# Two decoder-style layers on one core: the last tile's end on the VectorE, an expert merge by its transpose, and unread filler matmuls

## The chip, the cores and the metric

One core of a Trainium2 chip runs the whole program. The metric is the device time of one execution in microseconds (us), the median over runs. TensorE (PE) multiplies and transposes, VectorE (DVE) and GpSimd (POOL) do elementwise work, ScalarE (ACT) activations and copies, SyncE (SP) issues the stores. Each engine runs its instructions in the order in which the program lists them, and waits on semaphores where it must. GpSimd doesn't touch PSUM in this kernel.

## The reference

The input x has 4 batches of 512 tokens with 128 features; the context has 77 keys a batch.

```python
x = x + xattn0(layernorm(x), ctx, ctx, mask)      # 16 heads of 8, softmax over 77 keys, projection, biases
x = x + ffn0(layernorm(x))                        # 4-head attention over the batch axis, LN, 8-expert top-1 MoE with capacity, LN
x = x + xattn1(layernorm(x), ctx, ctx)            # 16 heads, only the 32 largest scores of 77 enter the softmax, values = ctx
x = x + ffn1(layernorm(x))                        # out = sigmoid(xr @ Wr.T) * (relu(xk @ Wk.T)**2 @ Wv.T), xr and xk mix a token with the one before
```

In the MoE an expert is two linear maps with no nonlinearity between them: `h = disp @ w1 + b1`, `y = h @ w2 + b2`. So an expert is one 128x128 matrix w1 @ w2 and one bias b1 @ w2 + b2. In xattn1 the cutoff is the 32nd largest score of a row, and `scores >= cutoff` stay.

## The kernel before

The 2048 tokens are 16 tiles of 128 (t = 4 * batch + j). The first half of the program works on the four tiles of one j at a time: `attend` (the first cross attention), `among` (attention over the batch axis, LN, the gate's logits) and `gates` (the place of a token in its expert, which needs the counts of the tiles before; for j = 3 those of all). The second half works by single tiles: `experts` (nine products with the merged experts, scaled on ScalarE and summed on TensorE), `query` and `kept` (LN, the queries, the scores in psS, their copy to SBUF), `topk`, `weigh`, `value` and `mix`.

Each engine's program is a set of small steps such as `max01@5`. The list `ORDER` names all steps of all engines in one row; `run` goes through it and emits, on each engine, the steps that this engine has. So the list alone decides what is queued behind what. Semaphores carry the data dependences, and `begun` counts in the list how many steps have used a PSUM bank before a given one.

`topk` of a tile is four rounds on the DVE: max (L897, 16 MAX8, one a head, the eight largest of 77) and, between them, mark (L905, MATCH_REPLACE8, which takes them out). `free` (L912) copies the largest of round 1 to mxc, `ends` (L916) the 32nd value. Then `weigh`: `dif` (L394, POOL) takes the maximum off the scores, `exp` (L582, ACT), `cut` (L400, POOL) takes the cutoff off, `sign` (L586, L588, ACT: sign, then relu) makes 0 or 1 of it, `product` (L407, POOL) multiplies both. `dif` waits for mx_copied, which `ends` sets, though it reads only what `free` wrote. `turn0` to `turn2` (L1184) transpose the 1232 weights of a token in ten chunks, `copy0` to `copy2` bring them to SBUF, `value` (L1198) multiplies with the context, `norm` (L925, L928, DVE) divides by the sum, `add3` (L417, POOL) adds x2. `mix`: `sum4`, `square4`, `scale4`, `norm4` are the LN on ACT and POOL with zf as result; `fturn` (L1211), `shift`, `up` (L1216 to L1219, four products), `acts`, `down` (L1223), `fvalue` (L627, ACT, a copy out of PSUM), `half` and `end` (L428, L431, POOL). SP stores fin.

The merge of the experts stands in j = 0: `wa0` to `wa7` (L1045) multiply w1 and w2 of an expert in four pieces of K = 128, `w12c` copies four results, and `bb0` to `bb7` (L1056) make b1 @ w2 of all experts with a weight matrix b1z that has one column set for each, 32 matmuls; `b12c` (L742) adds b2.

The product with the mask row (L978) has bf16 operands `mones` (ones) and `mrow` (the fill values, zero where the key is allowed).

## Time and profile before

| | us |
|---|---|
| median of three runs | 627.32 |
| the runs | 620.28, 627.32, 627.65 |
| the profiled execution | 621.48 |
| its span, first to last instruction | 619.7 |
| busy: PE, DVE, ACT, POOL | 424.8, 498.3, 284.2, 264.3 |

The profile is of one execution. Times in it count from the start of its span. "Busy" is the time in which an engine works; an instruction's idle time is the gap ahead of it, with what ended it. PEclk is the granted TensorE clock as a share of 2.4 GHz. An fp32 matmul stands as two records.

### The profile page before, as it was taken

How to read it: one execution, taken by the hardware profiler on the slowest of the kernel's cores; microseconds unless marked ns; L12 is line 12 of the kernel's file. 1: busy time of each engine (PE TensorE's matmuls, PEld its weight loads, DVE VectorE, ACT ScalarE, POOL GpSimd, SP SyncE). 2: the span in 40 equal slices, each digit the busy share in tenths (PEclk: the TensorE clock that was granted, in tenths of full speed). 3: DMA queues.
4: the chain of work that ended last, by engine and by line, in shares of the span. 5: the costliest groups of instructions: out<-in, count | busy, mean ns of one | idle time of the engine just before them, and what ended most of it. 6: DMA issues, size and time to landing. Idle time of an engine off the chain costs nothing.

```text
span 619.7 us, 10123 instructions
## 1 busy us (share of the span) xinstructions
PE 424.8 (69%) x2376; PEld 320.2 (52%) x2376; DVE 498.3 (80%) x3052; ACT 284.2 (46%) x786; POOL 264.3 (43%) x396
## 2 busy tenths in 40 slices
PE   4589987787777748236775876866797687455634
PEld 3359756674666435125654545655565465344523
DVE  5844669949587898989759999999989999989900
ACT  2214122324333224313675677666847766642342
POOL 4400300410240073523574476656747755663361
PEclk9669996969699577655878579877956886655555
DMA  8500000000000000000000000000000000000000
GB/s 285 223 1 1 1 2 1 1 0 2 2 1 1 2 1 1 0 2 1 1 5 5 2 6 5 2 5 6 5 2 5 6 2 5 5 6 5 5 2 8
DMA packets 6075, 9.56 MB, mean 15 GB/s; under 512 B 888, under 2 KB 5120, under 8 KB 5760
## 3 DMA queue, kind: packets, MB, share of 16 engines
q1 hardware_dynamic: 5728, 8.35, 3.8%
q10 hardware_dynamic: 288, 0.56, 0.3%
q8 instruction: 20, 0.33, 0.2%
q14 instruction: 39, 0.32, 0.2%
HBM read 7.86 MB, written 1.05 MB: 14 GB/s over the span
## 4 chain that ended last, share of the span: by engine, by line
PE 38%; DVE 18%; POOL 14%; ACT 14%; issue 14%; DMA 1%; SPq 0%; POOLq 0%; ACTq 0%; DVEq 0%
PE psM L1007 5%; PE psM L1150 4%; POOL dif L394 3%; PE psM L1198 3%; ACT area_b L586 3%; PE psM L1142 3%; POOL area_b L400 3%; PE psT L1184 3%; DVE area_b L905 2%; POOL p L407 2%; ACT mparts L545 2%; DVE d L673 2%; PE psM L1078 2%; DVE top L897 2%; PE psS L975 2%
## 5 line engine op out<-in xcount | busy, mean ns | idle before, releaser
L897 DVE MAX8 top<-area_b 128x8 f32<-128x77 f32 x768 | 112.3, 223 | 0.0
L905 DVE MATCH_REPLACE8 area_b<-top,area_b 128x77 f32<-128x77 f32 x512 | 106.8, 223 | 0.0
L307 POOL TENSOR_TENSOR rstd_m<-veps_m,expo 128x4 f32<-128x4 f32 x8 | 8.2, 1019 | 114.5 <-DVE veps_m L641 114.5
L1184 PE MATMUL psT<-consts,p 128*128 128x128 f32 (+1 forms) x160 | 37.7, 369 | 24.5 <-POOL p L407 18.8
L1007 PE MATMUL psM<-vblk,pT 128*128 128x81 f32 (+1 forms) x320 | 46.5, 309 | 10.4 <-DVE x L694 5.8
L905 DVE MATCH_REPLACE8 area_b<-top,area_a 128x77 f32<-128x77 f32 x256 | 53.5, 223 | 0.0
L407 POOL TENSOR_TENSOR p<-area_b 128x1232 f32<-128x1232 f32 x16 | 45.6, 2851 | 17.7 <-issue 13.2
L1198 PE MATMUL psM<-vblk,pT 128*128 128x81 f32 (+1 forms) x320 | 49.3, 321 | 4.6 <-ACT pT L600 4.2
L1198 PEld LDWEIGHTS psM<-vblk,pT 128*128 128x128 f32 (+1 forms) x320 | 48.0, 237 | 8.5 <-issue 7.1
L1007 PEld LDWEIGHTS psM<-vblk,pT 128*128 128x128 f32 (+1 forms) x320 | 45.4, 227 | 12.9 <-issue 12.5
L394 POOL TENSOR_TENSOR dif<-area_a,mxc 128x1232 f32<-128x1232 f32 x16 | 36.0, 2247 | 37.5 <-DVE mxc L916 37.5
L897 DVE MAX8 top<-area_a 128x8 f32<-128x77 f32 x256 | 37.5, 224 | 11.8 <-ACT area_a L574 11.4
L1142 PE MATMUL psM<-w,y1T 128*128 128x512 f32 (+1 forms) x64 | 32.7, 601 | 19.6 <-ACT mparts L545 19.4
L1184 PEld LDWEIGHTS psT<-consts,p 128*128 128x128 f32 (+1 forms) x160 | 24.9, 185 | 40.1 <-POOL p L407 23.6
L545 ACT ACTIVATE mparts<-psM,cur 128x128 f32<-128x128 f32 x128 | 38.0, 367 | 13.9 <-PE psM L1142 13.7
L1150 PE MATMUL psM<-mparts,consts 128*128 128x128 f32 x288 | 41.4, 307 | 0.0
L905 DVE MATCH_VALUE_LOAD area_b<-top,area_b 128x8 f32 x512 | 40.8, 80 | 0.0
L1150 PEld LDWEIGHTS psM<-mparts,consts 128*128 128x128 f32 x288 | 40.5, 226 | 0.0
L470 ACT ACTIVATE pT<-psT 128x512 f32<-128x512 f32 x16 | 9.6, 597 | 58.4 <-PE psM L1007 31.6
L400 POOL TENSOR_TENSOR area_b<-area_a,mxc 128x1232 f32<-128x1232 f32 x16 | 36.0, 2247 | 0.6
L582 ACT ACTIVATE area_b<-dif 128x1232 f32<-128x1232 f32 x16 | 19.7, 1230 | 33.6 <-POOL dif L394 33.5
L668 DVE TENSOR_REDUCE mx<-psS 128x16 f32<-128x1232 f32 x16 | 23.0, 1436 | 12.3 <-PE psS L978 12.3
(210 smaller groups left out, 1058.3 us busy)
## 6 DMA issues: line engine op xcount, KB each, us to landing
area_a<-in_w1T SPq DMA_DIRECT2D x1, 2048.0 KB, 10.7
area_b<-in_w SPq DMA_DIRECT2D x1, 2048.0 KB, 14.4
x<-in_x SPq DMA_DIRECT2D x4, 256.0 KB, 6.9
out<-fin SPq DMA_DIRECT2D x16, 64.0 KB, 1.5
rows<-in_rows SPq DMA_DIRECT2D x1, 576.0 KB, 7.5
vblk<-in_vblk SPq DMA_DIRECT2D x1, 540.0 KB, 15.2
weights<-in_weights SPq DMA_DIRECT2D x1, 516.0 KB, 6.6
consts<-in_consts ACTq DMA_DIRECT2D x1, 392.5 KB, 4.0
```

The source lines that it names most:

```text
L394: e.tensor_tensor(dif[:], scores_sb[t % RING][:], mxc[:, t % RING, 0, :, None].broadcast_to([P, H, KEYS]), ALU.subtract)\
L400: e.tensor_tensor(cut, scores_sb[t % RING][:], mxc[:, t % RING, 1, :, None].broadcast_to([P, H, KEYS]), ALU.subtract)\
L407: e.tensor_tensor(p1.rearrange("p (h k) -> p h k", k=KEYS), ex1, cut, ALU.mult).then_inc(s["p_set"], 1)
L545: ins = e.activation(mparts[:, x_], psM0[:, at + (x_ - lo) * D:at + (x_ - lo + 1) * D], ACT.Copy, scale=cur[:, D + x_:D + x_ + 1])
L668: e.tensor_reduce(mx0.rearrange("p (g i) -> p g i", g=G), scores_ps, AX, ALU.max).then_inc(s["s_max"], 1)
L897: ins = e.max(top[:, r, h], (left if r else scores_sb[t % RING])[:, h])
L905: ins = e.match_replace(left[:, h], top[:, r, h], (left if r else scores_sb[t % RING])[:, h], GONE)
L1007: ins = mm(pvs0[:, :, FIRST[c] * VE:FIRST[c] * VE + VB], pT[0:w, c], vblk0[0:w, b, c, None, :].broadcast_to([w, COPIES, VB]), start=(c == ...
L1142: mm(psM0[:, 0:(hi - lo) * D], y1T[:], w12[:, lo:hi].rearrange("p e n -> p (e n)"), start=True, stop=True)\
L1150: ins = mm(psM0[:, 0:D], ident, mparts[:, x_], start=False, stop=(x_ == E))
L1184: ins = tr(psT[0:w, 0, (c % 4) * P:(c % 4 + 1) * P], p1[:, c * P:c * P + w], ident)
L1198: ins = mm(pvs1[:, :, FIRST[c] * VE:FIRST[c] * VE + VB], pT1[0:w, c], vblk1[0:w, t // NJ, c, None, :].broadcast_to([w, COPIES, VB]), start ...
```

## The change

- **The last tile's end.** For t = 15 (`LASTT`) the steps `ends`, `cut`, `sign` and `product` are gone. Instead the DVE has `part0` to `part3`, four SCALAR_TENSOR_TENSOR each, `p = (score >= cutoff) * exp`, which read the cutoff straight from the fourth round of max. add3 and the LN of this tile go to the DVE (`close`: add, bn_stats, bn_aggr, add of epsilon; `closen`), with the power on POOL (`root`), and `end` reads the product from PSUM on the DVE, so that `fvalue` is gone for it.
- **dif.** It waits for S_read, set by `free`, and stands right behind `free` in the list; `cut` waits for mx_copied.
- **The merge by its transpose.** `wa` makes (w1 @ w2) transposed with b1 @ w2 as a 129th column, in three groups that ACT copies (`wt0` to `wt2`); `wu0`, `wu1` transpose four experts each back, `bu` the eight bias columns. b1z, b1T, its DMA and `bb` are gone. w1T carries b1 as a further row, made ahead on the host with the layout of the arrays.
- **Fillers.** `fill@0` to `fill@166` and `stoke@167` to `stoke@206` are each two matmuls with the operands of the mask row, whose result nothing reads. `fill` writes psT's second bank, and waits for the copies of what was there; `stoke` writes psS's last bank, once all scores are kept.
- **The list.** ORDER is written anew for all steps, before as much as after the places where the steps above stand.

The diff, with the parts cut that only delete declarations; of the list a line of either stands.

```diff
...
+LASTT = NT - 1
...
+FILLS = 167
+STOKES = 40
...
                 def a():
-                    hold(e, s["mx_copied"], t + 1)
+                    hold(e, s["S_read"], t + 1)
                     hold(e, s["exp_set"], t)
...
                     hold(e, s["p_set"], t)
+                    hold(e, s["mx_copied"], t + 1)
                     e.tensor_tensor(cut, scores_sb[t % RING][:], mxc[:, t % RING, 1, :, None].broadcast_to([P, H, KEYS]), ALU.subtract)\
...
 
-                return dict(dif=a, cut=b, product=c)
+                return dict(dif=a, cut=b, product=c) if t < LASTT else dict(dif=a)
 
...
                     e.tensor_tensor(x3[:, t % 2], x2[:, t % 8], att1[:], ALU.add).then_inc(s["x3_set"], 1)
-                return dict(add3=d)
+
+                def root():
+                    hold(e, s["z_step"], 3)
+                    e.tensor_tensor(rstd["m"][:, 0:1], veps["m"][:, 0:1], expo[:, 0:1], ALU.pow).then_inc(s["z_root"], 1)
+                return dict(add3=d) if t < LASTT else dict(root=root)
 
...
                     e.tensor_tensor(fin[:], x3[:, t % 2], vv, ALU.add).then_inc(s["f_fin"], 1)
-                return dict(scale4=ln_scalars(2, t, s["n4_sq"], s["n4_step"], s["n4_nm"]), half=one, end=end)
+                return dict(scale4=ln_scalars(2, t, s["n4_sq"], s["n4_step"], s["n4_nm"]), half=one, end=end) if t < LASTT else dict(half=one)
             run(e, attend=attend, among=among, experts=experts, query=query, weigh=weigh, value=value, mix=mix)
...
                 if j == 0:
+                    for n in range(3):
+                        def aside(n=n):
+                            lo, hi = 3 * n, min(3 * n + 3, E)
+                            e.wait_ge(s["w12_made"], n + 1)
+                            e.activation(w12t[:, lo:hi].rearrange("p e n -> p (e n)"), psM1[:, 0:(hi - lo) * (D + 1)], ACT.Copy)\
+                                .then_inc(s["w12t_copied"], 1)
+                        steps[f"wt{n}"] = aside
                     for n in range(2):
                         def keep(n=n):
-                            e.wait_ge(s["w12_made"], n + 1)
+                            e.wait_ge(s["w12_turned"], n + 1)
                             e.activation(w12[:, 4 * n:4 * n + 4].rearrange("p e n -> p (e n)"), psM1, ACT.Copy).then_inc(s["w12_stored"], 1)
...
                     return f
-                return dict(exp=a, sign=b, copy0=c(0), copy1=c(1), copy2=c(2))
+                steps = dict(exp=a, copy0=c(0), copy1=c(1), copy2=c(2))
+                if t < LASTT:
+                    steps.update(sign=b)
+                return steps
 
...
                     e.activation(vv, psT[:, 1, 3 * P:4 * P], ACT.Copy).then_inc(s["f_vv"], 1)
-                return dict(sum4=a1, square4=a2, norm4=a3, shift=shift, acts=acts, fvalue=value)
+                steps = dict(shift=shift, acts=acts)
+                if t < LASTT:
+                    steps.update(sum4=a1, square4=a2, norm4=a3, fvalue=value)
+                return steps
             run(e, attend=attend, among=among, experts=experts, query=query, kept=kept, weigh=weigh, mix=mix)
...
                 steps.update({f"mark{r}{g}": mark(r, g) for r in range(rounds - 1) for g in range(G)})
-                steps.update(free=free, ends=ends)
+                steps.update(free=free)
+                if t < LASTT:
+                    steps.update(ends=ends)
+                    return steps
+
+                def part(g):
+                    def f():
+                        hold(e, s["exp_set"], t + 1)
+                        hold(e, s["p_turned"], 3 * t)
+                        hold(e, s["topk_step"], last(2 * rounds - 2) + 1 + g)
+                        for h in range(g * HG, g * HG + HG):
+                            ins = e.scalar_tensor_tensor(p1[:, h * KEYS:(h + 1) * KEYS], scores_sb[t % RING][:, h], top[:, rounds - 1, h, 7:8],
+                                                         ex1[:, h], ALU.is_ge, ALU.mult)
+                        ins.then_inc(s["p_part"], 1)
+                    return f
+                steps.update({f"part{g}": part(g) for g in range(G)})
                 return steps
...
                                     rden1[:, :, None].broadcast_to([P, H, HD]), ALU.mult).then_inc(s["a_norm"], 1)
-                return dict(norm=a)
-            run(e, attend=attend, among=among, gates=gates, topk=topk, value=value)
+
+                def close():
+                    hold(e, s["f_fin"], t - 1)
+                    hold(e, s["n4_out"], t)
+                    hold(e, s["a_norm"], t + 1)
+                    e.tensor_tensor(x3[:, t % 2], x2[:, t % 8], att1[:], ALU.add).then_inc(s["x3_set"], 1)
+                    hold(e, s["x3_set"], t + 1)
+                    e.bn_stats(stats["m"][:, 0], x3[:, t % 2]).then_inc(s["z_step"], 1)
+                    hold(e, s["z_step"], 1)
+                    e.bn_aggr(mv["m"][:, 0], stats["m"][:, 0]).then_inc(s["z_step"], 1)
+                    hold(e, s["z_step"], 2)
+                    e.tensor_scalar(veps["m"][:, 0:1], mv["m"][:, 0, 1:2], EPS, None, ALU.add).then_inc(s["z_step"], 1)
+
+                def norm():
+                    hold(e, s["z_root"], 1)
+                    hold(e, s["f_turned"], t)
+                    e.tensor_scalar(zf, x3[:, t % 2], mv["m"][:, 0, 0:1], rstd["m"][:, 0:1], ALU.subtract, ALU.mult).then_inc(s["n4_out"], 1)
+                return dict(norm=a) if t < LASTT else dict(norm=a, close=close, closen=norm)
+
+            def mix(t):
+                def end():
+                    hold(e, s["f_one"], t + 1)
+                    hold(e, s["f_v"], t + 1)
+                    hold(e, s["f_fin"], t)
+                    e.tensor_tensor(vv, psT[:, 1, 3 * P:4 * P], er, ALU.mult).then_inc(s["f_mul"], 1)
+                    hold(e, s["f_mul"], t + 1)
+                    hold(e, s["stored"], 16 * t)
+                    e.tensor_tensor(fin[:], x3[:, t % 2], vv, ALU.add).then_inc(s["f_fin"], 1)
+                return dict(end=end) if t == LASTT else {}
+            run(e, attend=attend, among=among, gates=gates, topk=topk, value=value, mix=mix)
 
...
                                 e.wait_ge(s["v_masked"], 2 * B)
-                            if x_ == 4:
-                                e.wait_ge(s["w12_stored"], 1)
+                            if x_ % 3 == 0:
+                                hold(e, s["w12t_copied"], x_ // 3)
                             for c in range(FC):
-                                ins = mm(psM1[:, (x_ % 4) * D:(x_ % 4 + 1) * D], w1T[:, c, x_], w2[:, c, x_], start=(c == 0), stop=(c == FC - 1))
-                            if x_ % 4 == 3:
+                                ins = mm(psM1[:, x_ % 3 * (D + 1):(x_ % 3 + 1) * (D + 1)], w2[:, c, x_], w1T[:, c, x_],
+                                         start=(c == 0), stop=(c == FC - 1))
+                            if x_ in (2, 5, 7):
                                 ins.then_inc(s["w12_made"], 1)
...
 
-                    def bias(x_):
+                    def upright(n):
                         def f():
-                            if x_ == 0:
-                                e.wait_ge(s["w12_stored"], 2)
-                                e.wait_ge(s["b1_spread"], 1)
-                            for c in range(FC):
-                                ins = mm(psM1[0:E, 0:D], b1z[:, c, x_ * E:(x_ + 1) * E], w2[:, c, x_],
-                                         start=(x_ == 0 and c == 0), stop=(x_ == E - 1 and c == FC - 1))
-                            if x_ == E - 1:
-                                ins.then_inc(s["b12_made"], 1)
-                                e.wait_ge(s["weights_in"], 16)
+                            e.wait_ge(s["w12t_copied"], 3)
+                            hold(e, s["w12_stored"], n)
+                            for x_ in range(4):
+                                ins = tr(psM1[:, x_ * D:(x_ + 1) * D], w12t[:, 4 * n + x_, 0:D], ident)
+                            ins.then_inc(s["w12_turned"], 1)
                         return f
+
+                    def bias():
+                        e.wait_ge(s["w12_stored"], 2)
+                        tr(psM1[0:E, 0:D], w12t[:, :, D], ident).then_inc(s["b12_made"], 1)
+                        e.wait_ge(s["weights_in"], 16)
                     steps.update({f"vb{n}": spread(n) for n in range(2)}, **{f"wa{x_}": merged(x_) for x_ in range(E)},
-                                 **{f"bb{x_}": bias(x_) for x_ in range(E)})
+                                 **{f"wu{n}": upright(n) for n in range(2)}, bu=bias)
                 return steps
...
                     def f():
+                        if t == LASTT:
+                            hold(e, s["p_part"], min(2 * g + 2, G))
                         if g == 0:
-                            hold(e, s["p_set"], t + 1)
+                            hold(e, s["p_set"], min(t + 1, LASTT))
                             hold(e, s["t_copiedA"], 3 * begun(f"turn0@{t}", "ta0", "ta1", "ta2", "ta3"))
...
                     hold(e, s["t_copiedV"], begun(f"fturn@{t}", "tb0", "tb1", "tb2", "tb3"))
-                    hold(e, s["b1_spread"], 6)
+                    hold(e, s["mix_set"], 5)
                     tr(psT[:, 1, 0:P], zf, ident).then_inc(s["f_turned"], 1)
...
                 return dict(fturn=turn, up=up, down=down)
-            run(e, attend=attend, among=among, gates=gates, experts=experts, query=query, weigh=weigh, value=value, mix=mix)
+            def warm(k):
+                def stream(bank):
+                    for _ in range(2):
+                        mm(bank[:, 0:B * KEYS], mones[:], mrow.rearrange("p b k -> p (b k)"), start=True, stop=True)
+
+                def between():
+                    hold(e, s["v_masked"], 2 * B)
+                    hold(e, s["t_copiedV"], begun(f"fill@{k}", "tb0", "tb1", "tb2", "tb3"))
+                    hold(e, s["f_vv"], begun(f"fill@{k}", "fturn"))
+                    stream(psT[:, 1])
+
+                def after():
+                    hold(e, s["S_kept"], NT)
+                    stream(psS[:, G - 1])
+                return dict(fill=between) if k < FILLS else dict(stoke=after)
+            run(e, attend=attend, among=among, gates=gates, experts=experts, query=query, weigh=weigh, value=value, mix=mix, warm=warm)
 
...
 INDICES = dict(attend=range(NJ), among=range(NJ), gates=range(NJ), experts=range(NT), query=range(NT), kept=range(NT), topk=range(NT),
-               weigh=range(NT), value=range(NT), mix=range(NT))
-ORDER = """hstats@0 masks@0 hrstd@0 kblk1@0 hnorm@0 vb0@0 kblk@0 vb1@0 bias@0 vm0@0 hturn@0 hstats@1 keys@0 hT@0 vm1@0 hq@0 hrstd@1 wmix@0
-hqT@0 s0@0 hnorm@1 hstats@2 bias@1 hturn@1 hT@1 mx0@0 hq@1 hrstd@2 hnorm@2 sub0@0 bias@2 hstats@3 s1@0 exp0@0 hrstd@3 ta0@0 mx1@0
...
-keep@15 max00@14 dif@13 max01@14 sum4@12 max02@14 square4@12 max03@14 mark00@14 cut@13 exp@13 mark01@14 mark02@14 mark03@14
+mark13@15 exp@15 turn2@14 max20@15 copy2@14 max21@15 value@14 max22@15 max23@15 mark20@15 mark21@15 mark22@15 mark23@15 max30@15
...
         consts=consts, early=early, weights=weights, cols=cols, rows=rows, vblk1=laid.transpose(1, 2, 0, 3, 4).reshape(P, B, NCH, VB),
-        b1T=a["L0_ffn_b1"].reshape(E, FC, P).transpose(2, 1, 0),
         b2=a["L0_ffn_b2"],
-        w1T=a["L0_ffn_w1"].reshape(E, D, FC, P).transpose(3, 2, 0, 1),
+        w1T=np.concatenate([a["L0_ffn_w1"], a["L0_ffn_b1"][:, None, :]], axis=1).reshape(E, D + 1, FC, P).transpose(3, 2, 0, 1),
         w2=a["L0_ffn_w2"].reshape(E, FC, P, D).transpose(2, 1, 0, 3),
...
```

Three places of the list, as it comes out on an engine. First GpSimd (POOL) over one tile in the full stretch near the end; L400 (after: L401) is cut, L394 dif, L407 (L408) product, L417 (L418) add3, L359 to L363 scale4, L423 to L431 (L428 to L436) the end of the tile before. Before:

```order
L394 TENSOR_TENSOR dif<-area_a,mxc 128x1232
L417 TENSOR_TENSOR x<-x,att 128x128
L400 TENSOR_TENSOR area_b<-area_a,mxc 128x1232
L359 TENSOR_SCALAR lvar<-lsq 128x1
L361 TENSOR_TENSOR lrs<-lvar,expo 128x1
L363 TENSOR_TENSOR lnm<-lneg,lrs 128x1
L407 TENSOR_TENSOR p<-area_b 128x1232
L423 TENSOR_SCALAR er<-er 128x128
```

And now:

```order
L418 TENSOR_TENSOR x<-x,att 128x128
L401 TENSOR_TENSOR area_b<-area_a,mxc 128x1232
L359 TENSOR_SCALAR lvar<-lsq 128x1
L361 TENSOR_TENSOR lrs<-lvar,expo 128x1
L363 TENSOR_TENSOR lnm<-lneg,lrs 128x1
L408 TENSOR_TENSOR p<-area_b 128x1232
L428 TENSOR_SCALAR er<-er 128x128
L394 TENSOR_TENSOR dif<-area_a,mxc 128x1232
```

dif moved from ahead of the cut to behind the product; it is the next tile's dif there.

The DVE at the end of the program, before (L897 max, L905 mark, L925 and L928 norm, L916 ends):

```order
L905 MATCH_REPLACE area_b<-top,area_b 128x77 x16
L897 MAX top<-area_b 128x8 x16
L925 RECIPROCAL rden<-psM 128x16
L928 TENSOR_TENSOR att<-psM,rden 128x128
L916 COPY mxc<-top 128x16
L925 RECIPROCAL rden<-psM 128x16
L928 TENSOR_TENSOR att<-psM,rden 128x128
```

And now (L946 the parts, L966 to L977 close and closen, L985 and L988 end):

```order
L913 MAX top<-area_b 128x8 x8
L946 SCALAR_TENSOR_TENSOR p<-area_a,top,area_b 128x77 x4
L913 MAX top<-area_b 128x8 x8
L956 RECIPROCAL rden<-psM 128x16
L959 TENSOR_TENSOR att<-psM,rden 128x128
L946 SCALAR_TENSOR_TENSOR p<-area_a,top,area_b 128x77 x12
L956 RECIPROCAL rden<-psM 128x16
L959 TENSOR_TENSOR att<-psM,rden 128x128
L966 TENSOR_TENSOR x<-x,att 128x128
L968 BN_STATS stats_m<-x 128x6
```

The first part stands between two groups of max, the other three behind tile 14's norm.

TensorE around the routing of j = 3, before (L950 the turns, L1089 and L1100 products of `among`, L1118 and L1119 places, L1198 value of tile 0, L1127 and L1128 tile 3's turn):

```order
L950 MATMUL psM<-consts,oo 128x128 x4
L1089 MATMUL psM<-weights,mT 128x128 x4
L950 MATMUL psM<-consts,y1s 128x128 x4
L1100 MATMUL psM<-weights,mT 128x8 x4
L1118 MATMUL psM<-oh,consts 128x104
L1119 MATMUL psM<-seen_odd,ones 128x104
L1198 MATMUL psM<-vblk,pT 128x3x27 x10
L1127 MATMUL psM<-consts,cur 128x128
```

And now (L1291 the fillers):

```order
L1009 MATMUL psM<-consts,oo 128x128 x4
L1291 MATMUL psT<-mrow,mones 128x308 x6
L1150 MATMUL psM<-weights,mT 128x128 x4
L1291 MATMUL psT<-mrow,mones 128x308 x52
L1009 MATMUL psM<-consts,y1s 128x128 x4
L1291 MATMUL psT<-mrow,mones 128x308 x4
L1161 MATMUL psM<-weights,mT 128x8 x4
L1291 MATMUL psT<-mrow,mones 128x308 x28
L1179 MATMUL psM<-oh,consts 128x104
L1180 MATMUL psM<-seen_odd,ones 128x104
```

The same steps in the same order, with 45 pairs between them.

## Rows read from the trace of the kernel before

**Rows 1.** Windows of the whole span; columns as "us, PE PEld DVE ACT POOL busy (x), PEclk, DMA share, GB/s".

```profile
0.00:19.00 19.00, 9.12 (x50) 6.25 (x50) 11.20 (x41) 3.99 (x6) 9.30 (x23) 1.00 0.90 313
19.00:43.00 24.00, 16.30 (x69) 9.89 (x70) 16.59 (x40) 4.78 (x7) 5.76 (x11) 0.51 0.19 81
43.00:98.00 55.00, 48.66 (x389) 38.97 (x388) 33.73 (x64) 17.22 (x35) 5.64 (x10) 1.00 0.00 1
98.00:299.00 201.00, 137.81 (x726) 102.20 (x727) 165.93 (x718) 65.14 (x165) 59.55 (x75) 0.73 0.00 1
299.00:317.00 18.00, 12.27 (x80) 9.40 (x80) 7.74 (x63) 13.26 (x41) 11.17 (x17) 0.88 0.02 5
317.00:588.00 271.00, 187.99 (x1013) 143.59 (x1013) 261.94 (x2126) 169.05 (x506) 160.48 (x245) 0.73 0.02 4
588.00:619.70 31.70, 12.66 (x56) 9.85 (x55) 1.18 (x5) 10.73 (x29) 12.38 (x17) 0.55 0.02 5
```

**Rows 2.** Waits: engine, line, waited for; us in total, times, longest.

```profile
DVE rden L925 <- PE psM L1198: 25.6, 6, 18.5
...
DVE top L897 <- ACT area_a L574: 11.4, 2, 10.2
```

**Rows 3.** Timeline of the end: start us, us, engine, line, operation [idle before, releaser].

```profile
588.71 0.26 DVE L925 RECIPROCAL rden<-psM 128x16 f32<-128x16 f32 x1 [0.96 <-PE psM L1198]
...
589.46 2.25 POOL L394 TENSOR_TENSOR dif<-area_a,mxc 128x1232 f32<-128x1232 f32 x1 [7.15 <-DVE mxc L916]
...
597.38 0.47 PE L1211 MATMUL psT<-consts,zf 128*128 128x128 f32 x1 [8.70 <-ACT zf L526]
...
600.09 1.06 PE L1184 MATMUL psT<-consts,p 128*128 128x128 f32 x4
...
601.90 1.11 PE L1184 MATMUL psT<-consts,p 128*128 128x128 f32 x4
...
604.87 3.00 PE L1198 MATMUL psM<-vblk,pT 128*128 128x81 f32 x20 [0.73 <-ACT pT L600]
607.91 0.26 DVE L925 RECIPROCAL rden<-psM 128x16 f32<-128x16 f32 x1 [18.53 <-PE psM L1198]
...
611.84 0.48 PE L1211 MATMUL psT<-consts,zf 128*128 128x128 f32 x1 [3.97 <-ACT zf L526]
...
616.32 0.28 ACT L627 ACTIVATE vv<-psT 128x128 f32<-128x128 f32 x1 [0.89 <-PE psT L1223]
...
617.27 0.45 POOL L431 TENSOR_TENSOR fin<-x,vv 128x128 f32<-128x128 f32 x1
```

**Rows 4.** The page's groups (busy us, mean ns), and one round of max, tile 14's.

```profile
L905 DVE MATCH_REPLACE8 area_b<-top,area_b 128x77 f32<-128x77 f32 x512 | 106.8, 223 | 0.0
...
568.44 2.34 DVE L897 MAX8 top<-area_a 128x8 f32<-128x77 f32 x16
```

**Rows 5.** The group of the freeing copy, and the timeline around it, tiles 12 and 15.

```profile
L912 DVE COPY mxc<-top 128x16 f32<-128x16 f32 x16 | 8.6, 539 | 0.4
...
509.00 2.25 POOL L400 TENSOR_TENSOR area_b<-area_a,mxc 128x1232 f32<-128x1232 f32 x1
...
509.55 1.73 DVE L912 COPY mxc<-top 128x16 f32<-128x16 f32 x1
...
568.48 2.25 POOL L394 TENSOR_TENSOR dif<-area_a,mxc 128x1232 f32<-128x1232 f32 x1 [7.15 <-DVE mxc L916]
...
574.20 0.17 DVE L912 COPY mxc<-top 128x16 f32<-128x16 f32 x1
...
576.10 2.79 POOL L407 TENSOR_TENSOR p<-area_b 128x1232 f32<-128x1232 f32 x1 [1.57 <-issue]
```

**Rows 6.** Timeline of TensorE: the mask row's four matmuls at either clock.

```profile
40.21 1.21 PE L978 MATMUL psS<-mrow,mones 65*128 65x308 bf16 x4
...
50.65 0.70 PE L978 MATMUL psS<-mrow,mones 65*128 65x308 bf16 x4
```

**Rows 7.** The group of the bias products in the merge.

```profile
L1056 PE MATMUL psM<-area_b,b1z 128*8 128x128 f32 x64 | 7.5, 273 | 0.0
```

253 lines of the change are left out of this document (132 added, 121 removed).

## The prediction

> **What bounds the kernel now.** I read the table of windows first, then the list of waits, the timeline of the last 32 us, and then the rows of single instructions. In the windows the VectorE (DVE) is the engine to follow [rows 1]: it is busy for 498.3 of 619.7 us, and the 121.4 us in which it is not are 7.8 up to 19 us, 7.4 up to 43, 21.3 up to 98, 35.1 up to 299, 10.3 up to 317, only 9.1 in the 271 us of 317 to 588, and 30.5 at the end. So three things can shorten the program: a shorter end, fewer stalls ahead of 317 us, and fewer in the full stretch. TensorE is the reason for most stalls ahead of 299 us, and its granted clock says how it ran there: 0.51 in 19 to 43 and 0.73 in 98 to 299, where 0.5 is 1.2 GHz and 1.0 is 2.4 GHz.
>
> The waits name two places [rows 2]. The DVE waited 25.6 us for the product with the values (L1198), of which 18.5 is the last tile's and 7.1 are five waits of earlier tiles. It waited 10.2 us once for tile 3's scores: these need the routing of the last quarter, and only tile 2's top-k lies beside that chain.
>
> The end is a pure chain [rows 3]. The last MAX8 ends at 587.75 (the reciprocal at 588.71 less its 0.96 of idle); then come dif 589.46, first transposes 600.09, value 604.87, norm 607.91, turn of zf 611.84, copy of v 616.32, last add 617.27, end 619.7.
>
> **Part 1, the last tile's end.** Gone for tile 15: the copy of the cutoffs, the GpSimd's cut and product, ScalarE's sign and relu; dif and exp stand earlier, under the rounds of max. New: sixteen SCALAR_TENSOR_TENSOR on the DVE. The trace has none of 77 columns; below it stands MAX8, 2.34 us for 16 (0.146 each), above it MATCH_REPLACE8 with 106.8/512 = 0.209 [rows 4]. I take 0.16, the price nearest to a plain pass over 77 columns, with the ends 0.146 and 0.21 (2.3 to 3.4 us for all). Call M the end of the last MAX8. The first four now lie ahead of M (0.65 us later). Behind M: norm of tile 14 0.6, twelve parts 1.9. The first transposes need two parts: M+1.3, against M+12.3 before. The second group stood 1.8 behind the first [rows 3]: M+3.1 to M+4.2. Then tile 14's turn, the two last transposes (M+5.4) and, in front of value now, tile 14's four products (eight passes, 2 us at the 1.06 for four [rows 3]): value starts at M+7.5 instead of M+17.1. That is 9.6 less the 0.65, and I take off 0.9 because value may run at the low clock. The norm behind it goes by bn_stats, bn_aggr, an add, one GpSimd power and one DVE instruction, some 2.8 us instead of 611.84 - 607.91 = 3.9, and the last multiply reads PSUM on the DVE: 0.8 less. Sum: **-10**, bounds -7 to -12.
>
> **Part 2, dif ahead of the cutoff.** dif (2.25 us) waits for S_read instead of mx_copied, so behind the cutoffs only cut, sign, relu and product remain. The five waits of 7.1 us were at most 2.5 us long by the 25.6 less 18.5 [rows 2]; a chain 2.25 us shorter removes nearly all of them: **-5.5**, bounds 0 and -7.
>
> **Part 3, what it collides with.** The copy that frees the scores (L912) took 539 ns in the mean, 16 of them 8.6 us, though an undisturbed one takes 0.17: 5.9 us were lost. The rows of 509 us show how: GpSimd's cut runs from 509.00 to 511.25, the DVE's copy from 509.55 to 511.28 [rows 5]. The copy ends when the GpSimd instruction ends, and the DVE stands. In the last tiles of before the copy came at 574.20 and the product at 576.10, so they missed each other. With dif (started 568.48) gone from the front, the product starts some 2.3 us earlier, about 573.8, and runs for 2.8 us over the place of the copy: 2.0 to 2.4 us of stall in a tile. By the order of steps product@t-1 stands ahead of free@t for t = 5 and 9 to 15, eight tiles; for the others it stands behind. 8 x 1.6 = 13 less the 5.9 that are there: **+7**. Bounds: -6 (nothing collides) and +20 (thirteen tiles at 2.0, less 5.9). The Trainium skill says the same of the mechanism ("SBUF — State Buffer", Who interferes with whom): GpSimd and the DVE's second port pair are one lock, held for the whole instruction, and an fp32 copy may take it. It adds that who issues first wins. By that rule the product, issued first, blocks the copy, and the trace agrees with 1.73 against 0.17.
>
> **Part 4, fillers.** 167 pairs in psT's second bank, 40 in psS's last. The operands are those of the mask row, whose four matmuls took 1.21 us at the low and 0.70 at the high clock [rows 6]; so a pair costs about 0.6 or 0.35, and less where they follow each other. They cost nothing where TensorE would have waited, and cost their full time where the next instruction's operands are already there: TensorE goes in order. In 19 to 43 us TensorE was busy 16.3 of 24 us at 0.51 [rows 1]; at the high clock that is some 9.5, and the DVE's 7.4 of idle can fall by half: **-3.5** (0 to -6). In 98 to 299 the DVE idles 35.1 us at a mean clock of 0.73; a mean of 0.73 over two levels means 54% of the time at the low one, and that is where products take twice as long. I take **-8** (0 to -18). Tile 3's scores: products of some 13 us of TensorE at the low clock stand in that chain; half of that is 6, of which 5 shorten the 10.2: **-5** (0 to -10). Where a pair is in the way: TensorE's list has fillers at 38 places ahead of the last four tiles; if at twelve of them the operands come while a pair at the low clock is halfway, that is 12 x 0.3: **+4** (0 to +15). The last 34 pairs stand between value@11 and fturn@11; before, TensorE idled 8.7 us ahead of tile 14's turn of zf, the same place of a tile [rows 3]; they take 68 x 0.13 to 0.26 us. At the high price they'd delay tile 11's end by several us, but the top-k of tile 13 covers it: counted in the +4. None stands in the last three tiles, so the end isn't warmed by them.
>
> **Part 5, the merge.** 64 recorded passes of 7.5 us in one row go [rows 7], nine transposes and three ScalarE copies come, TensorE is left with some 5 us less in 43 to 98, where the DVE idles 21.3 us: **-3** (+1 to -5). One DMA less, one larger by 1/128, a memset and a small copy less: nothing, since the weights aren't waited for.
>
> **Sum.** -10 - 5.5 + 7 - 3.5 - 8 - 5 + 4 - 3 = -24, against the profiled execution's 621.5: 597.5. Its 621.5 stands 5.8 below the median of the three runs (627.3), which spread by 7.4. Moved by -24 the median would be 603.3. I forecast 600.
>
> **The rivals.**
> A. *The copies are blocked nearly everywhere and the clock gives little.* For: each steady tile has the same 6 us between the cutoffs and the next copy [rows 5]. Against: in tiles 6 to 8 the product stands behind. Part 3 at +16, part 4 at -8: about 614.
> B. *The clock gives what its stretches promise.* Part 4 at -28 and the chain of tile 3 gone, part 3 as forecast: 586. For: the two lowest clocks stand where the DVE idles. Against: shorter TensorE steps uncover ScalarE and GpSimd steps.
> C. *Only the end.* The order of steps brings ahead of 588 us as much as it takes (-10 alone): 611.5 by the profiled execution, 617 by the median, so about 2%.
> D. *Slower: pairs of fillers at the low clock in front of waiting steps.* If the clock doesn't follow, 167 pairs at 0.6 are 100 us of TensorE instead of 58, in order with the products that the DVE waits for. Part 4's gains (16.5) vanish and of the 100 us more than 40 would have to fall on the chain: 597.5 + 16.5 + 36 = 650. It decides from the point where the fillers delay the DVE by more than 20 us in all. Against: TensorE is idle for 63 of the 201 us of 98 to 299 [rows 1].
>
> **How the numbers follow.** Forecast 0.52, A 0.15, B 0.2, C 0.1, D 0.03. A measurement of this kernel can tell about 2% from no change, so faster means below 614.8. All of forecast and B, and half of A and C, lie below that: 0.85; within 2% 0.12; slower 0.03. The range takes in B and the nearer side of A: 585 to 616.
>
> **What would show it.** Right: the last MAX8 to the end 22 us instead of 32; copies of L928 (free) of 1.5 to 2.5 us in tiles 9 to 15 that end with GpSimd's product; no wait of norm over 0.5 us in the full stretch; granted clock over 0.9 in 215 to 317; the wait for tile 3's scores at 5 or less. Wrong: DVE idle ahead of 317 us above 80 (fillers in the way), or a steady tile that takes less than 20.7 us (no collision).

## The result, and the profile after

| | before | after |
|---|---|---|
| median, us | 626.1 (620.3, 627.3, 627.7, 624.9) | 639.18 (634.69, 642.47, 641.95, 636.42) |
| the profiled execution, its span | 621.48, 619.7 | 634.69, 632.8 |
| ratio | | 1.0268 [1.0213, 1.0322] |

The changed kernel is slower, by 2.7%; the forecast was 600, with 585 to 616 as its range. Medians here are over all runs of a kernel, ratios leave disturbed runs out, so the two need not agree to the last digit.

The same windows as [rows 1], with the borders moved to where the same work now stands:

```profile
0.00:19.00 19.00, 10.81 (x48) 7.23 (x49) 11.68 (x43) 3.99 (x6) 9.77 (x23) 0.86 0.91 320
19.00:43.00 24.00, 21.93 (x89) 11.86 (x87) 14.71 (x35) 4.09 (x7) 5.11 (x10) 0.50 0.18 75
43.00:98.00 55.00, 49.07 (x357) 41.33 (x358) 36.83 (x71) 19.56 (x40) 6.51 (x10) 0.90 0.00 1
98.00:299.00 201.00, 170.39 (x999) 124.11 (x999) 174.20 (x767) 68.39 (x175) 64.18 (x80) 0.82 0.00 1
299.00:335.00 36.00, 30.09 (x189) 20.64 (x189) 24.12 (x198) 24.55 (x82) 22.18 (x40) 0.95 0.02 5
335.00:600.00 265.00, 189.56 (x986) 142.92 (x984) 230.80 (x1854) 154.24 (x450) 146.98 (x217) 0.73 0.01 4
600.00:632.80 32.80, 18.21 (x74) 15.40 (x74) 16.23 (x110) 7.17 (x24) 4.63 (x11) 0.50 0.02 6
```

The sixth row tells the story. In 335 to 600 us the VectorE (DVE) is busy for 230.8 of 265 us, so it stands for 34.2; in the full stretch of before it stood for 9.1 of 271. The waits say for what, against 25.6, 6, 18.5 in [rows 2]:

```profile
DVE rden L956 <- PE psM L1261: 43.5, 8, 11.9
```

8.96 us of it is the last tile's; 34.5 is in other tiles, 2.1 at tile 1 and 32.4 behind ends@4. To date it, take the start of the copy of the cutoffs (`ends@t`), once a tile:

| `ends` of tile | 2 | 4 | 5 | 6 | 8 | 9 | 10 | 14 |
|---|---|---|---|---|---|---|---|---|
| before | 306.1 | 355.7 | 376.7 | 397.1 | 437.8 | 460.6 | 481.5 | 568.2 |
| after | 300.5 | 350.6 | 374.4 | 406.4 | 446.1 | 474.3 | 502.9 | 588.0 |

At tile 4 the changed kernel is 5.1 us ahead, at tile 14 it is 19.8 behind: 24.9 us are lost between them, all of it in the tiles that end at 374.4, 406.4, 474.3 and 502.9; the others take some 20 to 22 us as before. The end itself, timeline from the last MAX8 on (columns as in [rows 3]):

```profile
608.64 0.91 DVE L946 SCALAR_TENSOR_TENSOR p<-area_a,top,area_b 128x77 f32<-128x77 f32 x4
...
610.59 0.24 DVE L956 RECIPROCAL rden<-psM 128x16 f32<-128x16 f32 x1
...
611.07 2.79 DVE L946 SCALAR_TENSOR_TENSOR p<-area_a,top,area_b 128x77 f32<-128x77 f32 x12
...
612.25 1.12 PE L1247 MATMUL psT<-consts,p 128*128 128x128 f32 x4 [5.79 <-DVE p L946]
...
618.40 4.39 PE L1261 MATMUL psM<-vblk,pT 128*128 128x81 f32 x20
...
622.83 0.26 DVE L956 RECIPROCAL rden<-psM 128x16 f32<-128x16 f32 x1 [8.96 <-PE psM L1261]
...
625.70 0.48 PE L1274 MATMUL psT<-consts,zf 128*128 128x128 f32 x1 [2.40 <-DVE zf L977]
...
630.23 0.29 DVE L985 TENSOR_TENSOR vv<-psT,er 128x128 f32<-128x128 f32 x1 [4.59 <-PE psT L1286]
...
630.56 0.29 DVE L988 TENSOR_TENSOR fin<-x,vv 128x128 f32<-128x128 f32 x1
```

From 610.6 to 632.8 are 22.2 us, against 32.0: the end is as forecast. The groups that answer to [rows 4] and [rows 5], with the fillers:

```profile
L1291 PE MATMUL psT<-mrow,mones 65*128 65x308 bf16 x334 | 68.1, 359 | 1.3 <-DVE pT L698 1.3
...
L928 DVE COPY mxc<-top 128x16 f32<-128x16 f32 x16 | 10.7, 670 | 1.0
...
L946 DVE SCALAR_TENSOR_TENSOR p<-area_a,top,area_b 128x77 f32<-128x77 f32 x16 | 3.7, 302 | 0.0
```

The freeing copy lost 8.0 us (10.7 less 16 x 0.17), against 5.9. And at tile 13 it does just what the forecast said, ending with GpSimd's product (549.14 + 2.79 = 551.93, 549.43 + 2.53 = 551.96):

```profile
549.14 2.79 POOL L408 TENSOR_TENSOR p<-area_b 128x1232 f32<-128x1232 f32 x1 [1.57 <-issue]
549.43 2.53 DVE L928 COPY mxc<-top 128x16 f32<-128x16 f32 x1
```

### The profile page after: what moved, and what is told of

Read it like the earlier page. It is cut to its first block, busy times and chain, and to the rows that moved or that the text cites. A ratio compares the mean times of both kernels' runs of the same rounds, so it can differ in the third digit from the quotient of the medians.

```text
span 632.8 us, 11013 instructions
## 1 busy us (share of the span) xinstructions
PE 490.1 (77%) x2735; PEld 363.5 (57%) x2735; DVE 508.6 (80%) x3073; ACT 282.0 (45%) x781; POOL 259.4 (41%) x388
## 4 chain that ended last, share of the span: by engine, by line
PE 52%; DVE 25%; ACT 11%; issue 6%; POOL 4%; DMA 1%; SPq 0%; ACTq 0%; DVEq 0%; POOLq 0%
DVE area_b L921 8%; DVE top L913 7%; PE psM L1261 6%; PE psT L1291 5%; PE psM L1211 5%; PE psM L1066 4%; PE psM L1203 4%; PE psM L1198 3%; ACT mparts L557 3%; PE psT L1055 2%; PE psT L1247 2%; PE psS L1231 2%; PE psS L1034 2%; PE psM L1139 2%; PE psS L1037 1%
## 5 line engine op out<-in xcount | busy, mean ns | idle before, releaser
L1291 PE MATMUL psT<-mrow,mones 65*128 65x308 bf16 x334 | 68.1, 359 | 1.3 <-DVE pT L698 1.3
L1261 PEld LDWEIGHTS psM<-vblk,pT 128*128 128x128 f32 (+1 forms) x320 | 53.3, 259 | 10.0 <-issue 9.2
L1247 PE MATMUL psT<-consts,p 128*128 128x128 f32 (+1 forms) x160 | 35.7, 352 | 21.4 <-ACT pT L608 10.8
L1291 PEld LDWEIGHTS psT<-mrow,mones 65*128 65x128 bf16 x334 | 38.9, 118 | 23.0 <-issue 6.8
L408 POOL TENSOR_TENSOR p<-area_b 128x1232 f32<-128x1232 f32 x15 | 41.8, 2789 | 19.7 <-issue 12.5
L1066 PEld LDWEIGHTS psM<-vblk,pT 128*128 128x128 f32 (+1 forms) x320 | 41.5, 211 | 11.8 <-issue 11.6
L1203 PE MATMUL psM<-w,y1T 128*128 128x512 f32 (+1 forms) x64 | 35.8, 651 | 15.9 <-ACT mparts L557 15.8
L1247 PEld LDWEIGHTS psT<-consts,p 128*128 128x128 f32 (+1 forms) x160 | 24.1, 179 | 35.2 <-ACT pT L608 16.5
L1211 PE MATMUL psM<-mparts,consts 128*128 128x128 f32 x288 | 43.0, 315 | 0.0
L1211 PEld LDWEIGHTS psM<-mparts,consts 128*128 128x128 f32 x288 | 42.1, 233 | 0.0
L956 DVE RECIPROCAL rden<-psM 128x16 f32<-128x16 f32 x16 | 4.0, 250 | 43.5 <-PE psM L1261 43.5
L394 POOL TENSOR_TENSOR dif<-area_a,mxc 128x1232 f32<-128x1232 f32 x16 | 36.4, 2276 | 3.7 <-DVE mxc L928 3.6
L401 POOL TENSOR_TENSOR area_b<-area_a,mxc 128x1232 f32<-128x1232 f32 x15 | 33.7, 2248 | 8.1 <-DVE mxc L932 8.1
```

The source lines that it names most:

```text
L394: e.tensor_tensor(dif[:], scores_sb[t % RING][:], mxc[:, t % RING, 0, :, None].broadcast_to([P, H, KEYS]), ALU.subtract)\
L401: e.tensor_tensor(cut, scores_sb[t % RING][:], mxc[:, t % RING, 1, :, None].broadcast_to([P, H, KEYS]), ALU.subtract)\
L408: e.tensor_tensor(p1.rearrange("p (h k) -> p h k", k=KEYS), ex1, cut, ALU.mult).then_inc(s["p_set"], 1)
L1066: ins = mm(pvs0[:, :, FIRST[c] * VE:FIRST[c] * VE + VB], pT[0:w, c], vblk0[0:w, b, c, None, :].broadcast_to([w, COPIES, VB]), start=(c == ...
L1203: mm(psM0[:, 0:(hi - lo) * D], y1T[:], w12[:, lo:hi].rearrange("p e n -> p (e n)"), start=True, stop=True)\
L1211: ins = mm(psM0[:, 0:D], ident, mparts[:, x_], start=False, stop=(x_ == E))
```

## The stretch that went wrong, read in the trace

Tile 5 is the clearest. Around its value product:

```profile
393.03 1.06 PE L1247 MATMUL psT<-consts,p 128*128 128x128 f32 x4
...
397.03 0.49 PE L1203 MATMUL psM<-w,y1T 128*128 128x128 f32 x2 [0.65 <-ACT mparts L557]
...
399.79 3.61 PE L1211 MATMUL psM<-mparts,consts 128*128 128x128 f32 x18
...
403.46 2.36 PE L1261 MATMUL psM<-vblk,pT 128*128 128x81 f32 x20
...
405.85 0.26 DVE L956 RECIPROCAL rden<-psM 128x16 f32<-128x16 f32 x1 [11.91 <-PE psM L1261]
```

Between the first transposes of tile 5's weights (393.03) and their product with the values (403.46) TensorE works through the experts of tile 9: a product (L1203) that waits for ScalarE, and the sum (L1211), 3.61 us. And the DVE has nothing else to do, since in the new list norm@5 stands behind the last max of tile 6 and ahead of its `ends`; in the old one it stood one round later. Comparing the two lists gave three suspects:

- **N**: the norm of tiles 4, 5, 9, 10 and 11 is one round (some 6 us) earlier on the DVE. The waits are at norm@4, 5, 7, 8 and 9; norm@7 and norm@8 stand where they stood.
- **Q** and **V**: GpSimd's load and TensorE's total of tile t+4 stand ahead of cut and value of tile t. cut@5 came at 382.0, 7.6 us behind its `ends`, because load@9 in front of it waited 6.6 us for total@8.
- **B**: the experts are bunched. Between ends@4 and ends@6 the new list has total@7, 8 and 9, the old one total@7 and 8; between ends@8 and ends@9 it has total@12 and 13, the old one only total@11. The old list has such a pair too: total@12 and 13 between ends@9 and ends@10.

The tile windows of after, from ends@4 on, columns as in [rows 1]:

```profile
350.59:374.42 23.83, 18.85 (x106) 14.98 (x104) 20.21 (x166) 15.01 (x49) 14.02 (x23) 0.74 0.01 4
374.42:406.35 31.93, 24.84 (x126) 18.80 (x124) 19.85 (x165) 18.43 (x61) 14.92 (x26) 0.77 0.01 3
406.35:425.93 19.58, 13.16 (x64) 8.87 (x60) 19.41 (x164) 13.79 (x38) 12.91 (x21) 0.74 0.01 4
425.93:446.06 20.13, 14.22 (x81) 11.01 (x80) 20.03 (x165) 14.27 (x45) 13.95 (x22) 0.86 0.02 5
446.06:474.31 28.25, 24.16 (x107) 19.08 (x107) 20.31 (x166) 15.44 (x49) 13.99 (x23) 0.62 0.01 3
474.31:502.88 28.57, 21.99 (x114) 15.69 (x113) 19.84 (x166) 18.11 (x58) 14.65 (x25) 0.76 0.01 3
```

The DVE does the same 20 us of work in each. TensorE does 126, 107 and 114 matmuls in the long tiles and 64 and 81 in the short ones. Since the windows are cut by time, a tile that waits also collects more of them: the count alone doesn't say which is the cause.

## The experiments

Each was timed four times, e6, e8 and e10 ten times. `before`, timed again beside them, had medians of 622.7 to 624.6, against 626.1 above. Below, `after` is the changed kernel. Profiles are of one execution each.

**e1: no fillers.** Are the fillers in the way (rival D)?

```diff
-FILLS = 167
-STOKES = 40
+FILLS = 0
+STOKES = 0
```

(and no `fill` and `stoke` in the list)

> The changed kernel without the 207 filler pairs, everything else in its list as it was. Theory L (the new list is too tight in the full stretch: norm stands early on the DVE, cut behind load on GpSimd): the waits of norm for value stay at some 30 us ahead of the last tile, and the time stays at 633 to 642. Theory F (fillers stand in the way of TensorE, and by it value comes late): the waits of norm fall below 10 us and the time comes to 620 or less. Whatever the fillers gave ahead of 300 us goes: the cutoff copy of tile 2 later than 300.5 by up to 8 us.

Measured: 643.1 us, ratio 1.0303 [1.0246, 1.0361]. The loss is there without them (waits of 10.1, 5.9 and 5.8 us in the stretch, 39.7 in all), so they don't cause it. Theory L had it, the median 1.1 over its range; ends@2 came earlier (297.3), not later.

**e2: the old list from tile 5 on**, up to mark23@15, then the new end.

```diff
-ORDER: the new list
+ORDER: the new list to ends@4, what is left in the old list's order to mark23@15, the rest in the new one's
```

> The changed kernel with its own list up to the cutoff copy of tile 4 (fillers there included), then the list of before up to the third mark of tile 15, then its own end; no fillers in the last two parts. Theory L: from ends of tile 4 (350.6 in the changed kernel) to ends of tile 14 it takes the 212.5 us of before instead of 237.4, the end stays at 22 us behind the last MAX8, and the copies aren't blocked for 2.5 us: 606 to 612. Theory F: the fillers of the first part delay the expert chain, so the stretch stays long: over 620.

Measured: 611.57 us, ratio 0.9793 [0.9717, 0.987]. ends@4 at 355.2, ends@14 at 564.7: 209.5 us instead of 237.4, with one wait of 2.6. The tile windows from ends@4, against those above:

```profile
355.17:375.01 19.84, 12.36 (x84) 9.99 (x82) 19.74 (x164) 10.66 (x34) 9.74 (x16) 0.83 0.02 5
375.01:395.10 20.09, 14.94 (x84) 11.30 (x83) 19.99 (x164) 14.16 (x44) 13.77 (x22) 0.83 0.02 4
395.10:415.20 20.10, 14.10 (x84) 11.28 (x84) 20.00 (x165) 13.90 (x45) 13.36 (x21) 0.83 0.02 4
415.20:436.08 20.88, 14.94 (x86) 11.58 (x86) 20.78 (x165) 14.79 (x47) 14.04 (x22) 0.84 0.02 5
```

84, 84, 84 and 86 matmuls in these four; the six behind them have 96, 71, 100, 89, 82 and 49. The one with 100 is where the old list's own pair of totals runs (the 36 products L1211 of two tiles), and it isn't long, with 101 in before; after has 98 in a short tile too:

```profile
479.91:501.74 21.83, 16.68 (x100) 12.65 (x101) 21.73 (x164) 15.07 (x46) 11.20 (x17) 0.77 0.02 5
...
502.88:523.56 20.68, 15.37 (x98) 11.21 (x96) 19.90 (x165) 15.87 (x49) 14.14 (x23) 0.83 0.02 4
```

So a pair of totals in one tile isn't enough for a long tile. The edit is worth 27.6 us of median, more than the whole loss. It also takes out the 40 `stoke` pairs, which all stand behind ends@4. e1 and e6 below have no fillers at all and differ in the same order alone: 643.1 and 617.4 us, stretches of 246.4 and 217.9. The cause is the order of steps behind ends@4.

**e3: the freeing copy as a maximum over one element**, which gives the same value.

```diff
-                    e.tensor_copy(mxc[:, t % RING, 0], top[:, 0, :, 0]).then_inc(s["S_read"], 1)
+                    e.tensor_reduce(mxc[:, t % RING, 0], top[:, 0, :, 0:1], AX, ALU.max).then_inc(s["S_read"], 1)
```

> The changed kernel with the copy that frees the scores written as a max over one element (tensor_reduce) instead of a copy. Theory C (the copy is blocked by GpSimd's product): the three instances of 2.5 us fall to about 0.2, 7 us less at tiles 13 to 15, time 628 to 634. Theory L alone: the same, since it says nothing on these; if the form doesn't matter the three stay at 2.5 and the time at 639.

```profile
L928 DVE TENSOR_REDUCE mxc<-top 128x16 f32<-128x16 f32 x16 | 2.8, 177 | 1.0
```

All sixteen take 0.18 us, under GpSimd's instructions too: the stall is gone. But the waits of norm, in the list of waits, grew from 43.5 to 54.0:

```profile
DVE rden L956 <- PE psM L1261: 54.0, 10, 11.8
```

The profiled execution is no shorter, 633.0 us of span against 632.8. The median is, with 633.6 us (Theory C had 628 to 634), ratio 1.0106 [1.0029, 1.0183], below after's 1.0268 [1.0213, 1.0322]. So a part of the 7.9 us may be gained, 5.6 by the medians; the two profiles don't show where.

**e4: before, with the last tile's end alone** (and dif waiting for `free`, its place in the old list kept); merge, fillers and list of before.

```diff
-                    hold(e, s["mx_copied"], t + 1)
+                    hold(e, s["S_read"], t + 1)
...
-                return dict(dif=a, cut=b, product=c)
+                return dict(dif=a, cut=b, product=c) if t < LASTT else dict(dif=a)
...
+                steps.update({f"part{g}": part(g) for g in range(G)})
```

> The kernel before with part 1 alone (parts, close, closen, end on the DVE for tile 15), in the list of before up to the third mark of tile 15 with dif and exp of tile 15 behind product of tile 14, then the end of the new list. If the end gives the 10 us that the changed kernel's trace shows (from the last MAX8 to the end of the span 22.1 instead of 31.9): 9 to 11 us faster than before, 614 to 618. If it owes its size to the new list: less than 5.

Measured: 612.98 us, ratio 0.9815 [0.9767, 0.9863]. Two groups of its page are worth a look:

```profile
L928 DVE COPY mxc<-top 128x16 f32<-128x16 f32 x15 | 12.5, 836 | 0.3
...
L924 DVE COPY mxc<-top 128x16 f32<-128x16 f32 x16 | 8.0, 501 | 0.4
```

L928 is the copy of the cutoffs here, which took 0.17 us each in before. Dif no longer waits for it, so dif runs over it (dif 377.35 to 379.59, copy 377.75 to 379.63):

```profile
377.35 2.24 POOL L395 TENSOR_TENSOR dif<-area_a,mxc 128x1232 f32<-128x1232 f32 x1
377.75 1.88 DVE L928 COPY mxc<-top 128x16 f32<-128x16 f32 x1
```

12.5 less 15 x 0.17 is 9.9 us lost on this copy. The DVE's waits of over 0.4 us between ends@4 and ends@14 fell from 6.9 us to 0.8, but that stretch took 211.1 instead of 212.5: the two copies lost 11.1 us in it instead of 5.9.

**e5: the experts behind value**: in `after`, load to keep of tile t+4 behind value@t, for t = 5 to 9.

```diff
-... load@9 ... total@9 ... keep@9 ... value@5 ...
+... value@5 ... load@9 ... total@9 ... keep@9 ...
```

> The changed kernel, in whose list the expert, LN and query steps from load of tile t+4 on stand behind value of tile t, for t = 5 to 9; all other steps keep their order. In the changed list load and total of tile t+4 stand ahead of cut and value of tile t for t = 5 to 11, in the list of before value stands first up to t = 8. Theory X (what costs is that cut, sign, product, turns and value of a tile queue behind expert steps of four tiles later): the waits of norm in tiles 5 to 9, 28 us in the changed kernel, fall below 12, and the time to 615 to 626. Theory F2 (it isn't the experts but the stretch's other steps, LN and fillers): the waits stay above 20 and the time over 630.

Measured: 708.68 us, ratio 1.1463 [1.1316, 1.1609]. Waits of up to 35.6 us: the DVE now waited for scores as well. It fits F2's numbers, but the edit made a new shortage, so it tells neither theory from the other.

**e6: e2 without fillers**, **e7: e2 with e3's edit**, **e8: e2 with dif@t behind free@t and product@t-1** for t = 5 to 15.

> Run e2 without its fillers (they were all ahead of ends of tile 4). Theory K (the fillers keep the clock high and what follows gains): ends of tile 4 later by 5 to 10 us, time 616 or more. Theory N (they cost as much as they give: without them the changed kernel had ends of tile 2 at 297.3 instead of 300.5): ends of tile 4 within 3 us of 355, time 606 to 613.

Measured: 617.36 us over ten runs, ratio 0.9914 [0.986, 0.9969]. ends@2 came at 297.1, ends@4 at 348.2 (7 us earlier than in e2, where both theories had it later or the same), ends@4 to ends@14 took 217.9. The median is Theory K's.

> Run e2 with the freeing copy as a max over one element. Its copies took 8.9 us where sixteen undisturbed ones take 2.9. Theory C: 6 us less, 604 to 608. If the copies' stalls are made up for by shorter waits elsewhere: 610 to 613.

Measured: 611.92 us, ratio 0.9764 [0.9529, 0.9998]. The copies lost 0.1 us instead of 7.2; the waits in the stretch were 9.1 instead of 2.6. The median is the rival's; its runs lie between 600.6 and 614.8.

> Run e2 with dif of tiles 5 to 15 right behind free of its tile and product of the tile before, as in the changed list. Theory S (a chain shorter by 2.25 us helps): the one norm wait of 2.6 us goes and the time falls by 1 to 3, to about 609. Theory C (the product now starts ahead of the next free and blocks its copy): copies of 2 to 2.5 us in most tiles of the stretch, 8 to 15 us more, 618 to 626.

Measured: 615.74 us over ten runs, ratio 0.9828 [0.9745, 0.9911]. Not apart from e2, and neither theory: the waits of norm rose to 8.0 us, and of the copies only tile 15's was blocked for over 2 us (2.52; 1.3 to 1.6 at tiles 10 to 12).

**e9: `after` with the five norms later**, and **e10: e2 with them earlier**.

```diff
-... mark23@6 max30@6 max31@6 max32@6 max33@6 norm@5 ends@6 ...
+... mark00@7 mark01@7 mark02@7 mark03@7 norm@5 free@7 ...
```

> The changed kernel with one thing moved on the VectorE alone: the norm (division by the sum) of tiles 4, 5, 9, 10 and 11 stands where the old list has it, behind the first round of the tile after next (mark03@t+2), instead of one round earlier, behind the last max of tile t+1 and ahead of its ends. All other engines keep the new list. Theory N (the early place makes the cutoffs of tile t+1 wait for the value of tile t, so that two tiles that ought to overlap run one behind the other): the waits of 3.5, 11.9, 4.9 and 8.6 us in 317 to 588 shrink to at most 4 us in all, ends@14 is reached 209 to 216 us after ends@4 (237.4 in the changed kernel), and the median falls from 639 to 610-620. Theory Q (the value is late because on GpSimd load, and on TensorE total, of a later tile stand ahead of cut and value): the norm only waits at its new place, one round of some 6 us is all that is forgiven each time, the 11.9 leaves 6 and the 8.6 leaves 2.6 and both push the next tile again, ends@4 to ends@14 takes 222 or more, and the median is 622-632.

Measured: 639.46 us, of runs from 628.6 to 649.8; ratio 1.012 [1.002, 1.0221]. ends@4 to ends@14 took 232.6; the 11.9 of norm@5 fell to 2.3, but norm@6 waited 10.1 and norm@7 5.8, 26.9 us in the stretch. Theory N (4 us of waits, 209 to 216 us) fails. Q's 222 or more holds, its median doesn't.

> The opposite edit on the kernel whose full stretch has the old list (e2, 611.6 us, ends@4 to ends@14 209.5 us, one wait of 2.6): the norm of tiles 4, 5, 9, 10 and 11 one round earlier, behind the last max of tile t+1 and ahead of its ends, all else as in e2. Theory N: waits of 3 to 12 us come at those places, the stretch takes 222 to 238 us and the median is 622-640. Theory Q: with the old order on GpSimd and TensorE the value is there in time or up to 3 us late at each of the five, and nothing builds up: at most 8 us more in the stretch, median 611-620.

Measured: 625.81 us over ten runs, ratio 1.0037 [0.9987, 1.0087]; the stretch took 223.9, 14.4 more than in e2. Theory N had said 622 or more, and 222 to 238; norm@4 and norm@9 waited 4.2 and 5.6 us, the other three not. It isn't waits alone:

```profile
L928 DVE COPY mxc<-top 128x16 f32<-128x16 f32 x16 | 16.8, 1048 | 1.0
```

The freeing copies lost 14.1 us (7.2 in e2), the waits were 11.8 (2.6): 6.9 and 9.2, less 2.1 at the cutoffs' copy, make the 14.

**e11: `after` with load@9 behind cut@5 and load@14 behind cut@9.**

```diff
-... load@9 square2@8 cut@5 ...
+... square2@8 cut@5 load@9 ...
```

> The changed kernel with load@9 behind cut@5 and load@14 behind cut@9 on GpSimd, at the two places where cut waited 6.6 and 8.3 us behind a load that itself waited for total@8 and total@13. Nothing else is moved; the norms stay early. Theory Q: cut@5 comes at 374.5 instead of 382.0, cut@9 at 474.5 instead of 482.5, the waits of 11.9 (norm@5) and 8.6 (norm@9) fall below 5, and the median is 620-630. Theory N: sign, product and value of those tiles stand behind total and the other steps anyway, and any wait ahead of ends pushes all that follows: the waits add up to 20 or more still, median 634-643.

Measured: 644.24 us, ratio 1.034 [1.0266, 1.0414]. cut@5 now stood 0.7 us behind its `ends` instead of 7.6, and norm@5 still waited, for 13.0; value@5 ended 32.5 us behind ends@5 (31.4 in after). These two loads aren't it: Theory Q fails.

**e12: `after` with value@5 and value@9 right behind turn2 of their tile**, **e13: the same and e9's edit**.

```diff
-... turn2@5 ... lturn@8 copy2@5 total@9 ... ask@8 value@5 ...
+... turn2@5 value@5 ... lturn@8 copy2@5 total@9 ... ask@8 ...
```

> The changed kernel with value@5 and value@9 right behind turn2 of their tile on TensorE, ahead of lturn@8, total@9 and ask@8, and of fturn@8, total@14 and lturn@13. Nothing else is moved. Theory V (value late because the experts' sums of a later tile stand ahead of it on TensorE): value@5 starts some 3.8 us earlier than at 403.5, the wait of norm@5 falls from 11.9 to 8 or less and that of norm@9 from 8.6 to 5 or less, and the median falls from 639 to 627-634. Theory W (the time is lost by the order as a whole; what is moved ahead only makes the experts' sums late, and with them the next tiles): the sum of norm waits in 317 to 588 stays above 28 us and the median is 636-645.

Measured: 645.9 us, ratio 1.0342 [1.0233, 1.045]; waits of 43.6 us in the stretch, 11.5 of them at norm@5. Theory V falls; W has the waits, with the median 0.9 over its range. value@5 did start 2.6 us sooner behind ends@5 than in after, but took 4.5 us instead of 2.4, so its end moved from 31.4 to 31.0.

> The same with the five norms (tiles 4, 5, 9, 10, 11) one round later on the VectorE as in e9. Theory V with theory N (two causes that add up): waits of 317 to 588 at 12 us or less, median 612-626. Theory W: as e9, waits of 20 us or more that come up at other tiles (6, 7, 8), median 630-642.

Measured: 640.65 us, ratio 1.0271 [1.0174, 1.0369]; waits of 28.0 us, now at norm@5 (7.9), norm@6 (7.6) and three later ones. W holds.

**e14: e4 with e3's edit.**

> The kernel before with the last tile's end alone (e4, 613.0 us), and the freeing copy in the form of a maximum over one element, which took 0.18 us under a GpSimd instruction in e3. Theory C (what the copies lose is on the path): of the 5.9 us that the sixteen copies lose in the kernel before most comes back, median 606-610. Rival (the VectorE then stands that much longer for the norm, as in e7): median 611-615.

Measured: 613.8 us, ratio 0.9788 [0.9689, 0.9888], not apart from e4; its four runs (608.9, 609.3, 618.4, 621.9) don't decide between 606 to 610 and 611 to 615. The freeing copies lost 0.1 us instead of 5.3, and the waits rose from 0.8 to 7.6. With e3 and e7 this is the third profile in which the wait for value grew as the copies were freed.

**e15: e2's list with the new list kept to ends@7**, **e16: e2's list to ends@7 and then the new one**.

> Like e2, but the new list goes on to ends@7 and only then the old one follows. In the new list the experts of three tiles (total@7, total@8, total@9) stand between ends@4 and ends@6, in the old one those of two. Theory B (the loss is local: it comes in the tiles where the experts of more tiles are packed between two ends, TensorE is busy for 22 to 25 of some 29 us there, and norm, placed early, waits for value): ends@4 to ends@7 takes 72 to 78 us (75.3 in the changed kernel, 60.0 in e2), no wait over 3 us after it, and the median is 623-630. Theory G (no place in particular: a list is good or bad as a whole, and one whose two halves were not made for each other is worse): losses at the seam at tile 8 or behind it too, and the median is 632 or more.

Measured: 624.69 us (612.9 to 632.2, too spread for a ratio). ends@4 to ends@7 took 72.5 us, 60.0 in e2; the rest to ends@14 152.1, 149.5 in e2, with waits of 4.2 at the seam (norm@6) and 2.3 behind it. The length and the median are theory B's, its "no wait over 3 us" isn't. Up to ends@7 it has the early norms of tiles 4 and 5 as well as the bunch, and e10, with the early norms alone, took 68.6 us there.

> The complement: e2 (old list from tile 5 on) up to ends@7, and from there the new list, which packs total@12 and total@13 between ends@8 and ends@9 and has the norms of 8 to 11 early. Theory B: the waits of norm@8 and norm@9 come back (4.9 and 8.6 us in the changed kernel), ends@7 to ends@14 takes 158 to 166 us (162.1 in the changed kernel, 149.5 in e2), nothing is lost ahead of it, and the median is 620-628. Theory G: 632 or more, with waits at the seam.

Measured: 638.25 us, ratio 1.0213 [1.0147, 1.028]: outside what B gave (620 to 628), and what theory G gave (632 or more, with waits at the seam). ends@7 to ends@14 took 179.1, not 162. Its tile windows 7 to 9 show why:

```profile
408.49:428.34 19.85, 12.82 (x67) 8.32 (x68) 19.75 (x164) 10.34 (x36) 10.43 (x19) 0.81 0.02 5
428.34:472.12 43.78, 34.48 (x153) 26.39 (x152) 22.00 (x166) 26.25 (x76) 22.02 (x35) 0.62 0.01 2
472.12:500.55 28.43, 21.79 (x114) 15.48 (x113) 19.85 (x166) 18.14 (x58) 14.67 (x25) 0.76 0.01 3
```

In the new list total@10 stands ahead of ends@7, in the old one behind it, so at the seam four totals stand between ends@7 and ends@9, where the new list has three and the old one two; one tile got 153 matmuls and took 43.8 us, and norm@7 waited 16.8.

## Why the prediction was wrong

The step that failed is none of its five terms but what all of them were added to: it took the full stretch as it is in before ("only 9.1 in the 271 us of 317 to 588") and priced only the edits that have a name. "The list. ORDER is written anew for all steps" got a price of nothing beyond dif. It cost 27.6 us by e2 against after, and 25.7 by e6 against e1, with no fillers in either, in ten tiles. In its own terms: part 2 said that the norm's waits there would go; they rose from 7.1 to 34.5. A second step was mis-sized, the fillers (-16.5 and +4 against some -2 to -7, below); that is half or more of what e2 lacks to the forecast (611.6 against 600).

**What is shown of the cause.** Each row is ends@4 to ends@14 of one profiled execution; "copies" is what the two DVE copies into mxc lost over 0.17 us each in that stretch, "rest" what is left.

| us | stretch | DVE waits over 0.4 | copies | rest |
|---|---|---|---|---|
| before | 212.5 | 6.9 | 5.9 | 199.8 |
| e4, old list, new end | 211.1 | 0.8 | 11.1 | 199.2 |
| e2, old list behind ends@4 | 209.5 | 2.6 | 7.8 | 199.1 |
| e10, e2 with early norms | 223.9 | 11.8 | 12.4 | 199.7 |
| e9, after with later norms | 232.6 | 26.9 | 6.2 | 199.5 |
| after | 237.4 | 32.4 | 5.1 | 199.9 |
| e16 | 239.2 | 32.5 | 7.0 | 199.7 |

The rest is 199 to 200 us in each, as in the other kernels: the DVE's own work and nothing else. So the whole loss is wait for value, and the early norms alone bring 14 us on the old list.

A wait of norm has two sides: how long behind ends@t the value is ready, and when the DVE comes to norm@t. For tiles 5 and 9, first e2, then after (tile 5 of after stands above; its value ends at 405.82 and its ends@5 at 374.42):

```profile
396.30 2.35 PE L1261 MATMUL psM<-vblk,pT 128*128 128x81 f32 x20
400.89 0.25 DVE L956 RECIPROCAL rden<-psM 128x16 f32<-128x16 f32 x1
...
483.82 2.36 PE L1261 MATMUL psM<-vblk,pT 128*128 128x81 f32 x20
487.15 0.25 DVE L956 RECIPROCAL rden<-psM 128x16 f32<-128x16 f32 x1
...
499.91 2.43 PE L1261 MATMUL psM<-vblk,pT 128*128 128x81 f32 x20
502.38 0.26 DVE L956 RECIPROCAL rden<-psM 128x16 f32<-128x16 f32 x1 [8.55 <-PE psM L1261]
```

Tile 5: ready 23.6 us behind its `ends` in e2 and 31.4 in after, while the DVE was there at 25.9 and at 19.5. The value is 7.8 us later and norm 6.4 us earlier. Tile 9: ready at 27.2 and 28.0, the DVE there at 28.2 and 19.5; here the wait is the early norm's. But in e9, which moves both norms back, norm@5 and norm@9 waited 2.3 and 0 us and the stretch is only 4.8 us shorter: now value@6 and value@7 were ready 38.2 and 41.8 us behind their `ends` (24.5 and 28.9 in after). So late values and early norms both count, and taking one away moves the wait to other tiles.

What makes values late isn't shown. Bunched experts go with the long tiles (107 to 153 matmuls), but the old list has a pair of totals without loss, and e15's 12.5 us on the first bunch hold the early norms too. No kernel spreads the experts within the new list: e5, the one try, delayed them for good. Which engine's queue carries it stays open: GpSimd's two loads (e11) and the two places of value (e12) gave nothing by themselves.

**The end: right.** Forecast -10, measured 22.2 against 32.0 us from the last MAX8, less the 0.9 that the first four parts take ahead of it: -8.9. e4, the kernel with hardly more than that, is 1.4 to 2.3% faster, 9 to 14 us. Inside it two sizes were too small: a SCALAR_TENSOR_TENSOR took 0.91/4 = 0.23 us, not 0.16, above both ends of the range given (0.146 and 0.21), and value at the low clock 4.39 us instead of some 3.9. Both took from the gain, about 1 us in all.

**dif ahead of the cutoff: half right.** e4 shows its gain and its price apart: waits -6.1 (forecast -5.5), and 9.9 us on a copy that the forecast didn't look at, the one of the cutoffs. It weighed what dif's leaving does to `free`, not what dif's new start does to `ends`.

**The copies: the mechanism right, the term not.** Blocked copies end with GpSimd's product, at tiles 13, 14 and 15 (2.53, 2.52, 2.52 us), not in eight tiles: 2.1 us more than in before, not 7. +7 also had them all on the path. e3, e7 and e14 free them (7.9, 7.1 and 5.2 us). In e7 and e14 the medians stay where they were, and in all three profiles the DVE reaches norm earlier and waits there; e3's median fell by 5.6, so how much of such a stall is on the path isn't settled. The Trainium skill ("SBUF — State Buffer", Who interferes with whom) says that a reduction never takes the shared port pair, while a copy may; the runs agree, with 0.18 against 2.5 us under the same instruction.

**Fillers: too high.** Forecast -16.5 and +4. Ahead of tile 2's cutoffs they gave nothing and seem to cost some 5 us: ends@2 stood at 297.1 and 297.3 in the two kernels without them, and at 297.0 to 308.3, median 302.7, in the thirteen whose front is that of after. Tile 3's scores were waited for 10.7 us (10.2 before, forecast 5). The granted clock of 98 to 299 was 0.82, against 0.73 in before and in e1 without them, that of 215 to 317 was 0.77, against 0.66 and 0.64, not over 0.9, and in 19 to 43 it stayed at 0.50 with TensorE busy for 21.9 of 24 us. So the clock rose and the front didn't get shorter by it. What they gave comes later: e6 against e2, the stretch took 217.9 and 209.5 us, the median 617.4 and 611.6; e1 against after 643.1 and 639.2. That is -4 to -6 by the medians and -2 to -8 by the ratios, where the intervals of the first pair touch and those of the second overlap. Why matmuls that stand ahead of ends@4 shorten what follows is not settled; in 348 to 460 us the clock was 0.74 without them, in 355 to 460 0.81 with them.

**The merge** wasn't tried alone. With the new front and no fillers ends@2 stood at 297.1 and 297.3, with the old front at 306.1, 306.4 and 311.7 (before, e4, e14): 9 us or more of gain for the merge and the front's list together, of which fillers take back some 5.

**The rivals.** Rival C (only the end, 611 to 617) is what e4 and e2 measured. Rival D had the right sign and the wrong mechanism. None of the four had the list itself as the loss, though places of both lists were printed ahead of the prediction.

**The sum again**, from 626: the end -10 to -13, the front, merge and fillers 0 to -2 (611.6 of e2 against 613.0 of e4), the new list behind ends@4 +25.7, taken from e1 and e6 so that the result isn't in its own sum: 637 to 642, for 639.2.

## What to carry to other kernels

When a change rewrites an order written by hand, the order is a part of the change with a price of its own: for each step at which the bound engine waits, see how late its operand is ready and how early the engine comes to it, in either list. Here the order behind one step cost more than all named edits gave. Don't place an instruction that waits, on the engine that sets the time, ahead of work that is ready: five of them one round earlier cost 14 us on the good list (e10). Moving them back on the bad list gave little (e9), so mend an order as a whole or go back to the one that worked. And a stall in front of a wait need not be on the path: see whether the wait behind it grows when it goes.

## What the runs showed that was not expected

- A copy of 128x16 fp32 on the DVE took 0.17 us alone and up to 2.65 us under a GpSimd TENSOR_TENSOR; the same value by TENSOR_REDUCE took 0.18 at every place.
- The front varies between executions: ends@2 stood at 297.0 to 308.3 in thirteen kernels that have the same steps up to there (two of them, e3 and e7, with the other form of the freeing copy).
- TensorE at 91% busy (21.93 of 24 us) in 19 to 43 us had a granted clock of 0.50, and at 85% (170.39 of 201) one of 0.82.
- Stretch less waits less blocked copies is 199 to 200 us in all eighteen kernels, from 209 to 313 us of stretch: on the bound engine nothing else changed.
